# A graph network and expert layer: two buffers for the transposed incidence matrix, compared a graph ahead

## The chip, the cores and the metric

The kernel runs on one core of one Trainium2 chip. The metric is the device time of one execution in microseconds (us). The kernel before takes 750.67 us, the median of 3 runs (749.53 to 751.47). A core has five engines that run side by side and wait for each other by semaphores: PE (TensorE, matrix products), DVE (VectorE), ACT (ScalarE), POOL (GpSimd) and SP (SyncE, which here only starts DMA transfers).

## The reference, cut to what matters

For each of 16 graphs with 512 nodes and 256 features, two layers follow each other. H is the incidence matrix: 1 where adj is not 0.

```
def hypergraph_conv(x, adj, W, b):
    H = (adj != 0).astype(x.dtype)
    w = adj.reshape(N, -1)[:, :C]                     # first row of adj
    xw = einsum('ncd,hd->nch', x, W)
    Dn = 1 / einsum('nce,ne->nc', H, w)               # 0 where the sum is 0
    Be = 1 / H.sum(axis=1)
    m = Be[:, :, None] * einsum('nce,nch->neh', H, xw)
    return Dn[:, :, None] * einsum('nce,neh->nch', H, m) + b

gnn:  h = layer_norm(relu(hypergraph_conv(xn, adj, W1, b1)))      # xn = layernorm(x)
      x1 = x + hypergraph_conv(h, adj, W2, b2) + xn
ffn:  x2 = layernorm(x1)
      logits = x2 @ router_w + router_b; top 2 of 4 experts, softmax -> mask
      comb = sum_e mask_e * silu(x2 @ expert_w_e + expert_b_e)
      y = x2 + comb @ out_w + out_b
      out = x1 + norm_w * y / sqrt(mean(y*y) + 1e-6)
```

## The kernel before, in words

One graph is one pass of `body`. Its 512 nodes are four tiles of 128 rows. Every float32 factor is split in two float16 parts (names that end in h and l, for high and low): ACT writes the high part from PSUM, DVE the low part, and PE multiplies the pairs. H stands in SBUF as `h16` and its transpose as `ht16`, both float16. DVE makes them by comparing the loaded `adjin` and `adjtin` with 0 (`prep_h`, L741, and `prep_ht`, L745).

`body(g)` is a pipeline of two stages: it does the graph network (conv) of graph g and the expert layer (ffn) of graph f = g - 1, and prepares x and H of graph g + 1. `steps` (L221) writes out bodies 0, 1, 2 and the last one, and a hardware loop runs 3 to 14. The order on each engine is the order in which its `body` is written; there is no scheduler. Every engine runs its own list and waits for semaphores.

On PE, one body is in this order: the degrees (L1393, the first instruction of a graph), A1 = H^T times xn (L1405), D = H times w (L1418, the first that needs `ht16` of this graph), the transposes of x2 with the two halves of A2 = H times A1 between them (L1363, L1375), the router (L1440 to L1443), experts 0 and 1, A3 = A2 times W1 with the transposes of the mask after its third tile, expert 2, the mask's rows (L1308, which need the copy `mt` by ACT, L512), the other experts mixed with transposes and V = h times W2, the output product, U = H^T times V (with `h16`) and B3 = H times U (L1346, the last reader of `ht16`).

On DVE a body begins with x1 of graph f (L974) and its statistics, then `prep_ht(g)`, then the low part of A1 (`a1l`, L902), the output rows `yf` of an earlier graph, `xtl` (the low part of the turned x2, L1032), the small steps of D and of the router, and the mask. Near its end stand `xsl`, y, the low part of U (`ul`, L1132) and `prep_h(g + 1)`.

On SP (L256 to L274) the loads and copies of a body are queued in this order: x of the next graph into `xin`, adj into `adjin` once `h16` is made, the transposed adj into `adjtin` once `ht16` is made, `out` from x1, the copy of `xn` into `xb`, and the constant out_b into `x2o`. `xb` is a sum that is gathered by POOL's DMAs: xn, plus x, plus b2, plus vadd, and DVE reads it for x1. ACT's `prep_x` (L435), which writes the next graph's `xn` over the old one, waits until the copy of `xn` has landed.

Of the kernel before, what the change touches and what calls it, by code (L numbers as in the profile page):

```python
# [47 lines left out]
def build(nc, x, adj, adjt, wrow, w1t, b1, gamma, beta, w2t, b2, rw, rb, ew, eb, ow, ob, nw, out):  # L48
# [4 lines left out]
    CG = 2  # L53
    assert (C, D, DH, NE) == (512, 256, 512, 4)

    with ExitStack() as ctx:
# [60 lines left out]
        h16 = sb("h16", [P, CT, C], F16)  # L117
        ht16 = sb("ht16", [P, CT, C], F16)
        wcur = sb("wcur", [P, CT, 4], BF16)
# [101 lines left out]
        def steps(eng, body, tail):  # L221

            body(eng, 0, conv=True, ffn=False, late=False, prep=True)
            body(eng, 1, conv=True, ffn=True, late=False, prep=True)
            body(eng, 2, conv=True, ffn=True, late=True, prep=True)
# [10 lines left out]
        def _(sp):  # L236
# [18 lines left out]

            def body(sp, g, conv, ffn, late, prep):  # L256
                if prep:
                    sp.wait_ge(xn_dn, 4 * g + 4)
                    sp.dma_start(xin[:, :, :], x[g + 1]).then_inc(x_in, 16)
                    sp.wait_ge(h_made, g + 1)  # L260
                    sp.dma_start(adjin[:, :, :], adj[g + 1].rearrange("(t p) e -> p t e", p=P)).then_inc(adj_in, 16)
                    sp.wait_ge(ht_made, g + 1)
                    sp.dma_start(adjtin[:, :, :], adjt[g + 1].rearrange("(t p) c -> p t c", p=P)).then_inc(adjt_in, 16)
# [25 lines left out]
        def _(gp):  # L289
# [94 lines left out]

            def body(gp, g, conv, ffn, late, prep):
                f, q = g - 1, g - 2
# [45 lines left out]
        def _(act):  # L432
# [124 lines left out]

            def body(act, g, conv, ffn, late, prep):
                f = g - 1
# [163 lines left out]
        def _(dve):  # L723
# [18 lines left out]

            def prep_ht(g):
                dve.wait_ge(adjt_in, 16 * g + 16)
                TS(ht16[:, :, :], adjtin[:, :, :], 0.0, None, ALU.not_equal).then_inc(ht_made, 1)  # L745

# [246 lines left out]

            def body(dve, g, conv, ffn, late, prep):
                f, q = g - 1, g - 2
# [8 lines left out]
                if conv:  # L1004
                    if ffn:
                        prep_ht(g)
                    if not ffn:
                        prep_ht(0)
                        largest(a_turn, slice(W1, W1 + 1), 0, a_top)
                        setup_mag_b()  # L1010
# [245 lines left out]
        def _(pe):  # L1256
# [109 lines left out]

            def a2_half(g, half, ffn):

# [4 lines left out]
                for d in range(KD):  # L1373
                    for k in range(CG * half, CG * half + CG):
                        mm(bank[A2_BANK[d]][:, :], a1h[:, k, P * d:P * d + P], ht16[:, k, :],  # L1375
                           start=(k == 0), stop=False)
                        ins = mm(bank[A2_BANK[d]][:, :], a1l[:, k, P * d:P * d + P], ht16[:, k, :],
                                 start=False, stop=(k == CT - 1))
                    if half == 1:
                        ins.then_inc(a2_rdy, 1)  # L1380

            def body(pe, g, conv, ffn, late, prep):
                f = g - 1
                if conv:
# [31 lines left out]
                    for t in range(CT):  # L1416
                        for k in range(CT):
                            ins = mm(bank[D_BANK][:, 4 * t:4 * t + 4], ht16[:, k, P * t:P * t + P], wcur[:, k, :],  # L1418
                                     start=(k == 0), stop=(k == CT - 1))
# [7 lines left out]
                if conv:  # L1427
                    a2_half(g, 0, ffn)
                if ffn:
                    turned_x2(f, 1)  # L1430
                if conv:
                    a2_half(g, 1, ffn)
# [67 lines left out]
                if conv:  # L1500

                    incidence(g, B3_BANK, ht16, uh, ul, u_lo, 4, b3_rdy)

# [136 lines left out]
```

## Time and profile before

| what | value |
| --- | --- |
| median of 3 runs | 750.67 us (749.53 to 751.47) |
| the profiled execution | 751.47 us, of which the span is 749.9 us |
| busy in the span | PE 705.3 us (94%), DVE 652.2 (87%), ACT 495.0 (66%), POOL 288.4 (38%) |
| mean granted clock of PE | 0.985 of full speed |
| chain that ended last | DVE 29%, PE 26%, DMA 14% (DMA xb<-xn alone 13%), ACT 13%, issue 12% |

The span runs from the first to the last instruction; the rest of the run's time lies around it. The end of a matrix product is modelled in the trace, so two products in a row overlap in it; the distance between the starts of two products is the exact thing. A product of 512 columns follows the one before after 0.216 us, one of 256 columns after 0.109 us. In rows of a timeline the last bracket tells how long the engine was idle before the instruction and what ended that.

### The profile page before, as it was taken

What the parts mean: (1) busy time and instruction counts of PE and PEld (TensorE: products, weight loads), DVE (VectorE), ACT (ScalarE), POOL (GpSimd) and SP (SyncE); (2) the same over time, 40 slices, a digit from 0 to 9 for tenths busy, and PEclk for the clock granted to TensorE, in tenths of its full rate; (3) what the DMA queues carried; (4) which work ended last, traced back from release to release, by engine and by line L of the source; (5) the groups of instructions that cost most, each with busy time, mean ns of one, the idle gap of its engine ahead of it and who ended that gap; (6) DMA issues with size and microseconds to landing.
All of it is one profiled execution on the core that took longest, in us unless ns stands there. A gap on an engine that the chain in (4) does not pass through costs nothing.

```text
span 749.9 us, 16620 instructions
## 1 busy us (share of the span) xinstructions
PE 705.3 (94%) x5573; PEld 482.4 (64%) x5573; DVE 652.2 (87%) x1569; ACT 495.0 (66%) x971; POOL 288.4 (38%) x670
## 2 busy tenths in 40 slices
PE   4787999999999999999999999999999999999983
PEld 3364584766758486675858577584857768585671
DVE  4878888889898989989898899988899998988776
ACT  4655757667594856758585766858576685847562
POOL 4223334144353525444351434435153453524242
PEclk9988999999999999999999999999999999999997
DMA  8455538376583838657393765738385664727312
GB/s 290 169 110 201 113 89 239 67 225 131 162 178 94 240 64 229 135 172 164 90 245 60 237 122 182 154 105 231 62 247 111 202 134 129 184 64 184 58 29 56
DMA packets 42584, 111.65 MB, mean 149 GB/s; under 512 B 4160, under 2 KB 5312, under 8 KB 42560
## 3 DMA queue, kind: packets, MB, share of 16 engines
q0 software_dynamic: 13536, 41.42, 30.4%
q1 hardware_dynamic: 29024, 69.92, 28.3%
q8 instruction: 14, 0.23, 0.1%
q14 instruction: 10, 0.08, 0.0%
HBM read 69.91 MB, written 16.25 MB: 115 GB/s over the span
## 4 chain that ended last, share of the span: by engine, by line
DVE 29%; PE 26%; DMA 14%; ACT 13%; issue 12%; POOL 2%; SPq 2%; DVEq 0%; POOLq 0%; ACTq 0%
DMA xb<-xn 13%; PE bank L1261 5%; DVE comb L863 4%; PE bank L1263 4%; PE bank L1262 4%; PE bank L1346 4%; PE bank L1347 4%; DVE silu L859 4%; DVE hntl L878 3%; DVE z L867 3%; DVE ybn L980 2%; DVE x L974 2%; DVE h L741 2%; DVE ht L745 2%; ACT xsh L449 2%
## 5 line engine op out<-in xcount | busy, mean ns | idle before, releaser
L1261 PE MATMUL bank<-xth,ewh 128*128 128x512 f16 (+1 forms) x272 | 100.6, 370 | 2.1 <-DVE ewl L782 2.1
L1263 PE MATMUL bank<-xth,ewl 128*128 128x512 f16 (+1 forms) x272 | 100.7, 370 | 0.0
L1262 PE MATMUL bank<-xtl,ewh 128*128 128x512 f16 (+1 forms) x272 | 100.7, 370 | 0.0
L507 ACT ACTIVATE silu<-bank,ebcol,ksc 128x512 f32<-128x512 f32 x120 | 92.1, 769 | 7.3 <-PE bank L1263 7.2
L1261 PE MATMUL bank<-w2h,hnth 128*128 128x256 f16 x256 | 70.7, 276 | 3.3 <-DVE hntl L878 2.6
L1263 PE MATMUL bank<-w2h,hntl 128*128 128x256 f16 x256 | 70.5, 275 | 0.0
L1262 PE MATMUL bank<-w2l,hnth 128*128 128x256 f16 x256 | 70.5, 275 | 0.0
L548 ACT ACTIVATE a1h<-bank,be 128x256 f16<-128x256 f32 x64 | 26.8, 469 | 54.3 <-PE bank L1406 51.0
L654 ACT ACTIVATE uh<-bank,be 128x256 f16<-128x256 f32 x64 | 26.8, 470 | 53.4 <-PE bank L1347 53.4
L525 ACT ACTIVATE hnth<-bank 128x512 f16<-128x512 f32 x64 | 37.9, 592 | 33.3 <-PE bank L1315 33.3
L1405 PE MATMUL bank<-xsh,h 128*128 128x256 f16 x256 | 58.3, 277 | 0.9 <-DVE xsl L764 0.9
L372 POOL TENSOR_TENSOR yme<-yms,epsrms 128x4 f32<-128x4 f32 (+1 forms) x17 | 3.8, 224 | 143.7 <-ACT ysq L542 136.1
L1346 PE MATMUL bank<-uh,ht 128*128 128x256 f16 x256 | 56.9, 273 | 1.6 <-DVE ul L1132 1.6
L1406 PE MATMUL bank<-xsl,h 128*128 128x256 f16 x256 | 58.2, 277 | 0.0
L1346 PE MATMUL bank<-vh,h 128*128 128x256 f16 x256 | 56.9, 273 | 1.3 <-DVE vl L883 1.3
L1347 PE MATMUL bank<-vl,h 128*128 128x256 f16 x256 | 56.9, 273 | 0.0
L1347 PE MATMUL bank<-ul,ht 128*128 128x256 f16 x256 | 56.9, 273 | 0.0
L863 DVE TENSOR_TENSOR comb<-comb,silu 128x1024 f32<-128x1024 f32 x45 | 54.9, 1219 | 0.5
L859 DVE TENSOR_TENSOR silu<-silu,bank 128x1024 f32<-128x1024 f32 x45 | 54.6, 1214 | 0.0
L520 ACT ACTIVATE hn<-r,hnb,hrs 128x512 f32<-128x512 f32 x64 | 51.8, 809 | 2.7 <-POOL hnb L324 2.6
L1132 DVE SCALAR_TENSOR_TENSOR ul<-bank,be,uh 128x256 f16<-128x256 f32 x64 | 28.0, 480 | 27.8 <-ACT uh L654 27.8
L867 DVE SCALAR_TENSOR_TENSOR z<-bank,dna,b1b 128x512 f32<-128x512 f32 x64 | 46.7, 748 | 4.7 <-PE bank L1263 2.2
(248 smaller groups left out, 2138.3 us busy)
## 6 DMA issues: line engine op xcount, KB each, us to landing
adjin<-adj SPq DMA_DIRECT2D x16, 1024.0 KB, 5.3
adjtin<-adjt SPq DMA_DIRECT2D x16, 1024.0 KB, 6.2
xin<-x SPq DMA_DIRECT2D x16, 512.0 KB, 4.2
xb<-xn SPq DMA_DIRECT2D x16, 512.0 KB, 8.5
xb<-x POOLq DMA_DIRECT2D x16, 512.0 KB, 8.7
xb<-b POOLq DMA_DIRECT2D x16, 512.0 KB, 5.4
xb<-vadd POOLq DMA_DIRECT2D x16, 512.0 KB, 4.5
out<-x SPq DMA_DIRECT2D x15, 512.0 KB, 6.8
```

Source lines behind the costliest of these rows:

```text
L507: af(silu[:, i % 4, :], bank[E_BANK[i]][:, :], ACT.Silu, bias=ebcol[:, i:i + 1], scale=ksc[:, 2:3]).then_inc(silu_dn, 1)
L520: af(hn[:, t, :], r[:, t, :], ACT.Identity, bias=hnb[:, t:t + 1], scale=hrs[:, t:t + 1]).then_inc(hn_dn, 1)
L859: TT(src, src, m, ALU.mult).then_inc(comb_st, 1)
L863: TT(comb[:, :, :], comb[:, :, :], silu[:, 2 * (e % 2):2 * (e % 2) + 2, :], ALU.add).then_inc(comb_st, 1)
L867: STT(z[:, t, :], bank[A3_BANK[t]][:, :], dna[:, t:t + 1], b1b[:, :], ALU.mult, ALU.add).then_inc(z_dn, 1)
L1261: mm(outp, lh, rh, start=first, stop=False)
L1262: mm(outp, lh, rl, start=False, stop=False)
L1263: return mm(outp, ll, rh, start=False, stop=last)
L1346: mm(b, weights[:, k, P * e:P * e + P], hi[:, k, :], start=(k == 0), stop=False)
L1347: ins = mm(b, weights[:, k, P * e:P * e + P], lo[:, k, :], start=False, stop=(k == CT - 1))
L1405: mm(b, h16[:, k, P * e:P * e + P], xsh[:, k, :], start=(k == 0), stop=False)
L1406: ins = mm(b, h16[:, k, P * e:P * e + P], xsl[:, k, :], start=False, stop=(k == CT - 1))
```

## The change

There are now two buffers `ht16`, one for even and one for odd graphs, and `prep_ht(g + 1)` stands near the end of body g, ahead of `ul`, in place of `prep_ht(g)` near the beginning of body g. `body` gets an argument `odd`; the loop's pass now does two graphs (3 and 4, 5 and 6, ...), with six passes in place of twelve. On SP the copy of `xn` and the store of x1 stand ahead of the load of `adjtin`. PE's router waits for the first half of `xtl` and, ahead of its third tile, for the second.

```diff
-            with eng.Fori(3, N - 1) as g:
-                body(eng, g, conv=True, ffn=True, late=True, prep=True)
-            body(eng, N - 1, conv=True, ffn=True, late=True, prep=False)
+            with eng.Fori(3, N - 2, 2) as g:
+                body(eng, g, 1, conv=True, ffn=True, late=True, prep=True)
+                body(eng, g + 1, 0, conv=True, ffn=True, late=True, prep=True)
+            body(eng, N - 1, 1, conv=True, ffn=True, late=True, prep=False)
...
                     sp.wait_ge(h_made, g + 1)
                     sp.dma_start(adjin[:, :, :], adj[g + 1].rearrange("(t p) e -> p t e", p=P)).then_inc(adj_in, 16)
+                if ffn:
+                    f = g - 1
+                    sp.wait_ge(x1_dn, 4 * f + 4)
+                if conv:
+                    if not prep:
+                        sp.wait_ge(xn_dn, 4 * g + 4)
+                    sp.dma_start(xb[:, :, :], xn[:, :, :]).then_inc(xn_kept, 16)
+                if ffn:
+                    sp.dma_start(out[f], x1[:, :, :]).then_inc(x1_st, 16)
+                if prep:
                     sp.wait_ge(ht_made, g + 1)
                     sp.dma_start(adjtin[:, :, :], adjt[g + 1].rearrange("(t p) c -> p t c", p=P)).then_inc(adjt_in, 16)
-                if ffn:
-                    f = g - 1
-                    sp.wait_ge(x1_dn, 4 * f + 4)
-                    sp.dma_start(out[f], x1[:, :, :]).then_inc(x1_st, 16)
-                if conv:
-                    sp.wait_ge(xn_dn, 4 * g + 4)
-                    sp.dma_start(xb[:, :, :], xn[:, :, :]).then_inc(xn_kept, 16)
...
-                    if ffn:
-                        prep_ht(g)
...
                 if ffn and prep:
                     y_part(f, 0)
+                if prep:
+                    prep_ht(g + 1, 1 - odd)
                 if conv:
                     for e in range(CT):
...
-                    pe.wait_ge(xt_lo, 2 * f + 2)
                     for t in range(CT):
+                        if t % CG == 0:
+                            pe.wait_ge(xt_lo, 2 * f + t // CG + 1)
```

SP's order in the third body (graph 2), before; `xn_dn`, `h_made`, `ht_made` and `x1_dn` are the semaphores that ACT or DVE raise when `xn`, `h16`, `ht16` and x1 are written:

```order
L259 DMA xin<-x 128x1024 [waits xn_dn]
L261 DMA adjin<-adj 128x4x512 [waits h_made]
L263 DMA adjtin<-adjt 128x4x512 [waits ht_made]
L267 DMA out<-x 128x1024 [waits x1_dn]
L270 DMA xb<-xn 128x1024 [waits xn_dn]
L274 DMA x2o<-ob 128x1024 [waits y_dn]
```

The same body of SP in the changed kernel:

```order
L260 DMA xin<-x 128x1024 [waits xn_dn]
L262 DMA adjin<-adj 128x4x512 [waits h_made]
L269 DMA xb<-xn 128x1024 [waits x1_dn]
L271 DMA out<-x 128x1024
L274 DMA adjtin<-adjt 128x4x512 [waits ht_made]
L278 DMA x2o<-ob 128x1024 [waits y_dn]
```

The copy of `xn` moved past the load of `adjtin` and the store of x1, and it is held by x1 alone where it stood behind `ht_made`.

DVE at the end of the third body, before (`u_hi` is raised by ACT's high part of U, `x2o_dn` and `o_rdy` belong to y):

```order
L764 SCALAR_TENSOR_TENSOR xsl<-xn,xsh 128x1024 [waits xs_hi]
L896 SCALAR_TENSOR_TENSOR y<-bank,ksc,x2o 128x512 [waits x2o_dn,o_rdy]
L1132 SCALAR_TENSOR_TENSOR ul<-bank,be,uh 128x256 [waits u_hi]
L1132 SCALAR_TENSOR_TENSOR ul<-bank,be,uh 128x256
L1132 SCALAR_TENSOR_TENSOR ul<-bank,be,uh 128x256 [waits u_hi]
```

The same place of DVE in the changed kernel:

```order
L768 SCALAR_TENSOR_TENSOR xsl<-xn,xsh 128x1024 [waits xs_hi]
L900 SCALAR_TENSOR_TENSOR y<-bank,ksc,x2o 128x512 [waits x2o_dn,o_rdy]
L749 TENSOR_SCALAR ht_odd<-adjtin 128x2048 [waits adjt_in]
L1136 SCALAR_TENSOR_TENSOR ul<-bank,be,uh 128x256 [waits u_hi]
L1136 SCALAR_TENSOR_TENSOR ul<-bank,be,uh 128x256
L1136 SCALAR_TENSOR_TENSOR ul<-bank,be,uh 128x256 [waits u_hi]
```

The comparison of the transposed matrix for the next graph now stands between y and `ul`; it has left its place between the statistics of x1 and `a1l`.

## Rows read from the trace of the kernel before

**Rows 1.** Busy time of each engine in graphs 3 to 14: us, busy (instructions), PEclk.

```profile
151.35:671.92 520.57, 515.76 (x4131) 353.72 (x4129) 473.09 (x1129) 359.28 (x708) 210.16 (x481) 1.00 0.62 156
```

**Rows 2.** PE's timeline, first instruction of graphs 2, 8, 9, 15: start us, us.

```profile
106.52 0.44 PE L1393 MATMUL bank<-one,h 128*128 128x1 f16 x12
...
368.55 0.49 PE L1393 MATMUL bank<-one,h 128*128 128x1 f16 x14
...
411.54 0.42 PE L1393 MATMUL bank<-one,h 128*128 128x1 f16 x11
...
671.92 0.44 PE L1393 MATMUL bank<-one,h 128*128 128x1 f16 x12
```

**Rows 3.** PE's timeline, first mask row of graphs 8 and 9.

```profile
387.33 0.38 PE L1308 MATMUL bank<-mt,sel 128*128 128x512 f16 x1
...
431.21 0.39 PE L1308 MATMUL bank<-mt,sel 128*128 128x512 f16 x1 [0.54 <-ACT mt L512]
```

**Rows 4.** ACT's timeline, next graph's xn in graphs 8 and 9.

```profile
381.55 1.09 ACT L442 ACTIVATE xn<-xin,xnb,xrs 128x256 f32<-128x256 f32 x2
...
425.60 1.09 ACT L442 ACTIVATE xn<-xin,xnb,xrs 128x256 f32<-128x256 f32 x2 [1.08 <-DMA xb<-xn]
```

**Rows 5.** Who waited for whom: us in total, times, longest us.

```profile
ACT xn L442 <- DMA xb<-xn: 5.8, 9, 1.1
...
PE bank L1261 <- DVE hntl L878: 2.6, 12, 0.6
```

**Rows 6.** SP's timeline in graph 8.

```profile
372.40 0.38 SPq L263 DMA_DIRECT2D adjtin<-adjt  x1
...
373.49 0.48 SPq L270 DMA_DIRECT2D xb<-xn  x1
```

**Rows 7.** DVE's timeline in the first part of graph 8.

```profile
369.18 0.84 DVE L974 SCALAR_TENSOR_TENSOR x<-bank,dnb,xb 128x256 f32<-128x256 f32 x2
...
371.18 1.19 DVE L745 TENSOR_SCALAR ht<-adjtin 128x2048 f16<-128x2048 f32 x1
...
373.86 0.87 DVE L902 SCALAR_TENSOR_TENSOR a1l<-bank,be,a1h 128x256 f16<-128x256 f32 x2
...
376.10 1.27 DVE L1032 SCALAR_TENSOR_TENSOR xtl<-bank,xth 128x512 f16<-128x512 f32 x2
```

**Rows 8.** PE's timeline in graph 8, last product of A2 and first of the router.

```profile
376.99 0.38 PE L1377 MATMUL bank<-ht,a1l 128*128 128x512 f16 x1
377.43 0.18 PE L1261 MATMUL bank<-rwh,xth 128*128 128x4 f16 x1
```

**Rows 9.** Timelines of graph 1: PE at D, ACT at x2, PE at expert 0.

```profile
60.96 0.55 PE L1418 MATMUL bank<-wcur,ht 128*128 128x4 bf16 x16 [1.14 <-DVE ht L745]
...
62.56 1.09 ACT L555 ACTIVATE x<-x,ynb,yrs 128x256 f32<-128x256 f32 x2 [1.12 <-POOL ynb L324]
...
70.32 0.61 PE L1261 MATMUL bank<-xth,ewh 128*128 128x512 f16 x1 [2.08 <-DVE ewl L782]
```

**Rows 10.** Line 270, the copy of xn into xb, all 16.

```profile
DMA to landing us min/median/max: 3.9/8.5/10.2
```

**Rows 11.** ACT's timeline in graph 8, second pair of a1h.

```profile
372.64 0.84 ACT L548 ACTIVATE a1h<-bank,be 128x256 f16<-128x256 f32 x2
```

**Rows 12.** POOL's timeline in graph 8, the same step for both halves of x1.

```profile
369.34 0.19 POOL L319 TENSOR_TENSOR yve<-ymv,epsln 128x2 f32<-128x2 f32 x1 [0.43 <-DVE ymv L984]
...
371.34 1.08 POOL L319 TENSOR_TENSOR yve<-ymv,epsln 128x2 f32<-128x2 f32 x1 [0.60 <-DVE ymv L984]
```

**Rows 13.** DVE's timeline at the end of graph 7, around the new place.

```profile
361.51 0.74 DVE L896 SCALAR_TENSOR_TENSOR y<-bank,ksc,x2o 128x512 f32<-128x512 f32 x1
363.50 0.88 DVE L1132 SCALAR_TENSOR_TENSOR ul<-bank,be,uh 128x256 f16<-128x256 f32 x2 [1.25 <-ACT uh L654]
```

**Rows 14.** DMA queues: packets, MB, share; and an issue: count, KB, us to landing.

```profile
q8 instruction: 14, 0.23, 0.1%
...
wf<-wrow SPq DMA_DIRECT2D x1, 32.0 KB, 1.9
```

More of the change, by code:

```diff
@@ L53, in build @@
     CG = 2
-    assert (C, D, DH, NE) == (512, 256, 512, 4)
+    assert (C, D, DH, NE) == (512, 256, 512, 4) and N % 2 == 0
     with ExitStack() as ctx:
@@ L221, in steps @@
         def steps(eng, body, tail):
-            body(eng, 0, conv=True, ffn=False, late=False, prep=True)
-            body(eng, 1, conv=True, ffn=True, late=False, prep=True)
-            body(eng, 2, conv=True, ffn=True, late=True, prep=True)
-            with eng.Fori(3, N - 1) as g:
-                body(eng, g, conv=True, ffn=True, late=True, prep=True)
-            body(eng, N - 1, conv=True, ffn=True, late=True, prep=False)
+            body(eng, 0, 0, conv=True, ffn=False, late=False, prep=True)
+            body(eng, 1, 1, conv=True, ffn=True, late=False, prep=True)
+            body(eng, 2, 0, conv=True, ffn=True, late=True, prep=True)
+            with eng.Fori(3, N - 2, 2) as g:
+                body(eng, g, 1, conv=True, ffn=True, late=True, prep=True)
+                body(eng, g + 1, 0, conv=True, ffn=True, late=True, prep=True)
+            body(eng, N - 1, 1, conv=True, ffn=True, late=True, prep=False)
             tail(eng)
@@ L254, in _, with body @@
                 sp.dma_start(dst, src).then_inc(c_in, 16)
-            def body(sp, g, conv, ffn, late, prep):
+            def body(sp, g, odd, conv, ffn, late, prep):
                 if prep:
@@ L383, in _, with body @@
             prep_x(0, again=False)
-            def body(gp, g, conv, ffn, late, prep):
+            def body(gp, g, odd, conv, ffn, late, prep):
                 f, q = g - 1, g - 2
@@ L556, in x2_part, with body @@
                        scale=yrs[:, t:t + 1]).then_inc(x2_dn, 1)
-            def body(act, g, conv, ffn, late, prep):
+            def body(act, g, odd, conv, ffn, late, prep):
                 f = g - 1
@@ L741, in prep_h, with prep_ht @@
                 TS(h16[:, :, :], adjin[:, :, :], 0.0, None, ALU.not_equal).then_inc(h_made, 1)
-            def prep_ht(g):
+            def prep_ht(g, odd):
                 dve.wait_ge(adjt_in, 16 * g + 16)
-                TS(ht16[:, :, :], adjtin[:, :, :], 0.0, None, ALU.not_equal).then_inc(ht_made, 1)
+                TS(ht16[odd][:, :, :], adjtin[:, :, :], 0.0, None, ALU.not_equal).then_inc(ht_made, 1)
             def prep_x_stats(g, tiles=range(CT)):
@@ L992, in degrees, with body @@
                 v.reciprocal(be[:, :], dmax[:, :]).then_inc(be_dn, 1)
-            def body(dve, g, conv, ffn, late, prep):
+            def body(dve, g, odd, conv, ffn, late, prep):
                 f, q = g - 1, g - 2
@@ L1365, in turned_x2, with a2_half @@
                 ins.then_inc(xt_rdy, 1)
-            def a2_half(g, half, ffn):
+            def a2_half(g, odd, half, ffn):
                 pe.wait_ge(a1_lo, 4 * g + CG * half + CG)
@@ L1374, in a2_half @@
                     for k in range(CG * half, CG * half + CG):
-                        mm(bank[A2_BANK[d]][:, :], a1h[:, k, P * d:P * d + P], ht16[:, k, :],
+                        mm(bank[A2_BANK[d]][:, :], a1h[:, k, P * d:P * d + P], ht16[odd][:, k, :],
                            start=(k == 0), stop=False)
-                        ins = mm(bank[A2_BANK[d]][:, :], a1l[:, k, P * d:P * d + P], ht16[:, k, :],
+                        ins = mm(bank[A2_BANK[d]][:, :], a1l[:, k, P * d:P * d + P], ht16[odd][:, k, :],
                                  start=False, stop=(k == CT - 1))
@@ L1380, in a2_half, with body @@
                         ins.then_inc(a2_rdy, 1)
-            def body(pe, g, conv, ffn, late, prep):
+            def body(pe, g, odd, conv, ffn, late, prep):
                 f = g - 1
@@ L1427, in body @@
                 if conv:
-                    a2_half(g, 0, ffn)
+                    a2_half(g, odd, 0, ffn)
                 if ffn:
@@ L1431, in body @@
                 if conv:
-                    a2_half(g, 1, ffn)
+                    a2_half(g, odd, 1, ffn)
                     if not ffn:
```

12 lines of the change are left out of this document (6 added, 6 removed).

## The prediction

> **What bounds the kernel now.** I read the busy times by stage first, then PE's timeline at the start of each graph, then what stands in front of PE's pauses, then the engines and transfers behind those.
>
> PE runs at its full level, 2.4 GHz, through graphs 3 to 14 and is busy for 515.8 of 520.6 us [rows 1]. So only what removes a pause of PE counts there, and the pauses are few. Two graphs show it: graph 8 begins at 368.55 and graph 9 at 411.54, a period of 42.99 us, and from graph 2 to graph 15 the mean is (671.92 - 106.52) / 13 = 43.49 [rows 2]. The slower graphs lose at one place above all. In graph 9 the first mask row on PE comes after an idle 0.54 us, waiting for ACT's copy mt [rows 3]. In graph 8 the same row has no pause. The reason is on ACT: its xn starts 13.00 us after the start of graph 8, and 14.06 after the start of graph 9, where it waited 1.08 for the copy xb<-xn to land [rows 2, 4]; mt stands behind xn in ACT's order. Nine graphs wait so, for 5.8 us together [rows 5]. The copy is late since it is issued at 373.49, behind the load that waits for ht [rows 6].
>
> Two small pauses are in every graph. Between the last product of A2 (376.99) and the router (377.43) lie 0.44 us, 0.22 more than a product takes: PE waits for xtl, which DVE ends at 376.10 + 1.27 = 377.37 [rows 7, 8]. The other is the wait of V for hntl, short each time [rows 5]. Graph 1 has larger ones: 1.14 for ht and 2.08 for ewl, both from DVE [rows 9].
>
> **The copy of xn.** The last x1 on DVE ends at 369.18 + 0.84 = 370.02 [rows 7]. SP can issue the copy about 0.3 later, at 370.3, 3.2 us earlier than now [rows 6], and ahead of 1.5 MB that stand before it now. Even the slowest landing of the 16, 10.2 us, brings it to 380.5 [rows 10]; with the median, 8.5, it is there at 378.8. ACT wants it at 381.2 (below). So the wait goes in every graph, with 0.7 us left in the worst case. Behind it on SP stand the store of x1, the load of adjtin and x2o's constant. They go out earlier as well, since ht was made a graph ago. The load of adjtin has until the end of the body, some 30 us.
>
> If all 13 periods from graph 2 on were like graph 8's, they would be 565.40 - 13 x 42.99 = 6.5 us shorter. The first of them, graph 2, also loses to hntl (the longest of those waits is 0.6) [rows 5], which the copy doesn't cause alone; I leave 0.4 with it and take -6.1 (bounds 0 and -6.5).
>
> **The comparison moved away from the start.** It takes 1.19 us of DVE [rows 7]. Little of this arrives further down, since the next wait takes over: the second pair of a1h on ACT ends at 372.64 + 0.84 = 373.48 [rows 11], and the second a1l, which needs it, stands at 373.86 [rows 7], so it can come 0.36 earlier, at 373.5. These 0.36 go on to xtl, to D, to vadd on ACT, to silu, to xn (381.55 becomes 381.2) and to the mask. For the router xtl then ends at 377.01, before PE wants it at 377.21, so its pause of 0.22 goes: 13 x 0.22 = -2.9 us (bounds 0 and -2.9). The wait by halves is a second way to the same 0.22 (the first half of xtl is there 0.6 before the second), and it can't be gained twice.
>
> The mask row gets no new pause with that: against graph 8, which has none [rows 3], PE arrives 0.22 earlier and mt comes 0.36 earlier. The wait for hntl stays: it is a chain of a transpose on PE, ACT's hnth and DVE, which moves with PE. So my floor for a period is 42.99 - 0.22 = 42.77.
>
> POOL shows one more thing: the step yve takes 0.19 us for the first half of x1 and 1.08 for the second, which starts 0.16 after DVE's ht did and ends as that ends [rows 7, 12]. At its new place ht meets no step of POOL in a graph of the loop, so the second half's statistics come 0.9 earlier. This is inside the 0.36, because ACT's a1h pair is next. The Trainium skill has the rule for it (SBUF — State Buffer, Who interferes with whom): a tensor_scalar of DVE in a two-port mode takes the port pair that it shares with GpSimd, and the second comer is blocked until the first is done. The trace agrees, with 1.08 against 0.19. The rule speaks against the change in one place: in graph 0 ht now falls on POOL's issue of xb<-vadd.
>
> **The comparison in its new place.** y ends at 361.51 + 0.74 = 362.25, and ul starts at 363.50 after 1.25 us of idleness, for ACT's uh [rows 13]. The comparison takes 1.19 [rows 7] and fits with some 0.1 left. That idleness is its cover; without it each graph would pay up to 1.1 us, 14 times, and PE's B3 would wait. I take 0, bounds 0 and +0.1 a graph. No one waits for the comparison itself until D of the next graph.
>
> **Graph 1.** D waits 1.14 us for ht, which is now made in body 0. PE can't use all of it, because x2 and ewl are late behind. There the comparison and POOL's blocked steps hold up ACT's x2 by 1.12 [rows 9]; ACT's x2, ewh and xth and DVE's xtl and ewl follow each other without a gap up to PE's 70.32. x2 can start when the second pair of a1h is done, 1.1 us earlier, and ewl ends 1.1 earlier. Value -1.1; bounds 0 and -1.3. PE is at its lower level, 1.2 GHz, after this pause and will be again.
>
> **Graph 0 and the end.** In body 0 the comparison falls in a similar idle gap of DVE. What it can cost is a later xb<-vadd and with it x1 of graph 0: 0 to +0.6; I take 0. The last body's chains are not touched.
>
> **The loop of two graphs.** Fewer returns save nothing that I can see: the last B3 product and the next graph's first instruction on PE follow each other as usual within the loop. I take 0 (a cost is the third rival).
>
> The sum is -6.1 - 2.9 - 1.1 = -10.1 us. From the profiled execution, 751.47 (span 749.9 and 1.6 around it), that is 741.4; it is the slowest of the three shown, and from the median, 750.67, it is **740.6**.
>
> **Rivals.** First, a floor at 42.99: something else of about 0.2 us (hntl's chain, or ul, if the comparison overruns its gap) takes the place of the router's pause. For it speaks that DVE is busy for 473.1 of the 520.6 us [rows 1] and gets its comparison back into the one real gap; against it that the pauses are seen and belong to xtl. Then 740.6 + 2.9 = 743.5.
>
> Second, the copy doesn't come earlier in effect: it now shares the queue with adjin's megabyte, which is issued just before it, and the landing stays near 381.5 to 382.5, or another transfer waits instead. Then -6.1 is lost and part of the router's -2.9: about 748 to 750. Against it speaks that the slowest landing still fits [rows 10].
>
> Third, slower: the loop's code no longer stays with the engines. A graph is (4131 + 4129) / 12 = 688 instructions on PE, so the pass grows to 1,376. The trace shows 14 instruction transfers of 16 KB on q8 over the whole span [rows 14], which is about one pass over the written code and no reload in twelve loop passes. If the doubled pass is past what is kept, the target of each of the 5 returns must be fetched. The shortest landing of a load is 1.9 us [rows 14]; PE and DVE would both pay, one behind the other, 5 x 3.8 = 19, less 5 x 0.7 that hides in DVE's and PE's slack: 740.6 + 15.5 = 756.1. It decides from 12.4 us on, 2.5 a return, since less would only eat the gain.
>
> The Trainium skill (Runtime: NRT & Kernel Launch, Instruction fetch mechanics) says two things here. One: PE's instruction memory holds 2,048 instructions and the others' 512, in blocks of 256; by this the pass fits, and the sum stands. The other: only two lines are kept, and a taken branch out of the two-page window forces a fetch. By that the loop of before, 2.7 pages of PE, would already fetch at every return, and the trace agrees with the first: 14 transfers in all. An estimate from that page puts the new pass at 5.4 of 8 pages, which leaves room, though not plenty.
>
> **Chances.** The forecast has 0.53 (739 to 742.5), the floor at 42.99 0.26 (742.5 to 746), the copy in vain 0.09, a reload of code 0.10, and 0.02 for a gain beyond the bounds. The range 738.5 to 747 holds the first two. About 0.3%, 2.3 us, is what a measurement here can tell from no change. Faster by more than that (under 748.4): the first two, the gain beyond and a third of the copy in vain, 0.84. Within it: 0.06, the rest of that case. Slower: the code, 0.10.
>
> **What would show it.** In the changed profile graphs 2 to 14 should be 42.8 us apart, all alike, with no wait of ACT for xb<-xn and none of PE for mt; the router's first product should follow A2's last after 0.22; the idle gap before ul should be 0.1 in place of 1.25, and the ul rows at the same distance from uh; yve should take 0.19 in both halves; D in graph 1 should have no wait. q8 should have two or three transfers more, as the written code is longer, and none between the loop's first and last pass. I am wrong if periods alternate between two lengths (the returns), or if the wait before B3 for ul has grown.

## The result, and the profile after

The changed kernel takes 742.42 us, the median of 4 runs (741.57 to 744.01), beside 750.9 us (749.53 to 751.47) for 4 runs of the kernel before. The ratio is 0.9892, 95% interval 0.9869 to 0.9914: 8.1 us, or 1.1%, faster. Run once more among the experiments it took 742.57 us, ratio 0.9899 (0.9881 to 0.9916). The profiled execution took 741.57 us with a span of 740.0; it is the fastest of its four, as the profiled 751.47 of before is the slowest of its four.

Graphs 3 to 14, as one stretch (its ends, then the columns of [rows 1]), and PE's first instruction of graphs 2, 8, 9 and 15, which answer to [rows 2]. The last number of such a row is how many of the degree's 16 products the trace has in a row:

```profile
149.33:662.57 513.24, 511.88 (x4131) 355.89 (x4129) 476.75 (x1129) 357.67 (x708) 203.51 (x481) 1.00 0.63 159
```

```profile
106.45 0.54 PE L1397 MATMUL bank<-one,h 128*128 128x1 f16 x16
...
363.23 0.42 PE L1397 MATMUL bank<-one,h 128*128 128x1 f16 x11
...
405.99 0.37 PE L1397 MATMUL bank<-one,h 128*128 128x1 f16 x9
...
662.57 0.39 PE L1397 MATMUL bank<-one,h 128*128 128x1 f16 x10
```

Graph 8 lasts 405.99 - 363.23 = 42.76 us, and so does every graph from 4 on. From graph 2 to graph 15 it is 556.12 us, 9.28 less than before. The rest of the difference between the two profiled executions (751.47 - 741.57 = 9.90) is: the start 0.22 later, graph 0 longer by 1.65 (42.52, now 44.17), graph 1 shorter by 1.94 (51.14, now 49.20), the part from graph 15 on shorter by 0.55 (78.0, now 77.4).

Graph 8 of the changed kernel, in the order of [rows 3, 4, 6, 7, 8]: ACT's xn and mt, the first mask row on PE, SP's queue, DVE's low parts, and A2's last product with the router's first.

```profile
375.74 1.09 ACT L446 ACTIVATE xn<-xin,xnb,xrs 128x256 f32<-128x256 f32 x2
...
380.72 0.57 ACT L516 ACTIVATE mt<-bank 128x512 f16<-128x512 f16 x1
...
381.78 0.38 PE L1312 MATMUL bank<-mt,sel 128*128 128x512 f16 x1
...
364.83 0.48 SPq L269 DMA_DIRECT2D xb<-xn  x1
365.50 0.44 SPq L271 DMA_DIRECT2D out<-x  x1
366.04 0.72 SPq L274 DMA_DIRECT2D adjtin<-adjt  x1
...
368.19 0.88 DVE L906 SCALAR_TENSOR_TENSOR a1l<-bank,be,a1h 128x256 f16<-128x256 f32 x2
...
370.44 1.27 DVE L1034 SCALAR_TENSOR_TENSOR xtl<-bank,xth 128x512 f16<-128x512 f32 x2
...
371.67 0.38 PE L1381 MATMUL bank<-ht_even,a1l 128*128 128x512 f16 x1
371.89 0.17 PE L1265 MATMUL bank<-rwh,xth 128*128 128x4 f16 x1
```

The copy goes out 1.60 us after the graph's start (4.94 before), no row of xn waits for it in any graph, mt is done at 381.29, half a microsecond before PE wants it, and the router follows A2 after 0.22. SP's line L269 now lands in a median of 4.2 us, against 8.5 in [rows 10]:

```profile
DMA to landing us min/median/max: 2.9/4.2/11.0
```

The comparison at its new place on DVE, which answers to [rows 13], and POOL's two steps yve, which answer to [rows 12]:

```profile
398.95 0.74 DVE L900 SCALAR_TENSOR_TENSOR y<-bank,ksc,x2o 128x512 f32<-128x512 f32 x1
399.61 1.22 DVE L749 TENSOR_SCALAR ht_odd<-adjtin 128x2048 f16<-128x2048 f32 x1
400.95 0.88 DVE L1136 SCALAR_TENSOR_TENSOR ul<-bank,be,uh 128x256 f16<-128x256 f32 x2
...
364.12 0.19 POOL L323 TENSOR_TENSOR yve<-ymv,epsln 128x2 f32<-128x2 f32 x1 [0.53 <-DVE ymv L988]
...
366.08 0.19 POOL L323 TENSOR_TENSOR yve<-ymv,epsln 128x2 f32<-128x2 f32 x1 [0.57 <-DVE ymv L988]
```

The gap of 1.25 us is filled, ul starts 2.00 us after y does (1.99 before), and yve takes 0.19 both times. One pause of PE is left in a graph of the loop, ahead of V's fourth tile. The last product of the third tile and the first of the fourth in graph 8:

```profile
394.68 0.27 PE L1267 MATMUL bank<-w2h,hntl 128*128 128x256 f16 x1
395.06 0.28 PE L1265 MATMUL bank<-w2h,hnth 128*128 128x256 f16 x1
```

They start 0.38 us apart, where 0.11 is usual: 0.27 for hntl.

Graph 1, PE's pauses, which answer to [rows 9]: D has none, but ewl's is longer (2.46, before 2.08), since PE arrives there earlier.

```profile
62.63 0.66 PE L1367 MATMUL bank<-ident,x 128*128 128x128 f32 x4 [0.57 <-ACT x L559]
68.05 0.16 PE L1265 MATMUL bank<-rwh,xth 128*128 128x4 f16 x1 [0.71 <-DVE xtl L1034]
71.46 0.61 PE L1265 MATMUL bank<-xth,ewh 128*128 128x512 f16 x1 [2.46 <-DVE ewl L786]
```

### The profile page after: what moved, and what is told of

Read it like the earlier page. It is cut to its first block, busy times and chain, and to the rows that moved or that the text cites. A ratio compares the mean times of both kernels' runs of the same rounds, so it can differ in the third digit from the quotient of the medians.

```text
span 740.0 us, 16405 instructions
## 1 busy us (share of the span) xinstructions
PE 699.6 (95%) x5573; PEld 485.1 (66%) x5573; DVE 656.4 (89%) x1569; ACT 493.0 (67%) x971; POOL 280.5 (38%) x670
## 4 chain that ended last, share of the span: by engine, by line
PE 26%; DVE 21%; issue 18%; POOL 11%; ACT 11%; DMA 9%; SPq 2%; POOLq 1%; DVEq 0%; ACTq 0%
DMA x2o<-ob 8%; PE bank L1350 6%; PE bank L1351 6%; DVE comb L867 5%; DVE silu L863 4%; PE bank L1265 4%; PE bank L1267 3%; PE bank L1266 3%; POOL hrs L326 3%; DVE hntl L882 2%; ACT hn L524 2%; POOL xb L355 2%; DVE x L978 2%; ACT silu L511 2%; POOL hve L323 1%
## 5 line engine op out<-in xcount | busy, mean ns | idle before, releaser
L511 ACT ACTIVATE silu<-bank,ebcol,ksc 128x512 f32<-128x512 f32 x120 | 92.4, 770 | 10.5 <-PE bank L1267 9.7
L882 DVE SCALAR_TENSOR_TENSOR hntl<-bank,hnth 128x512 f16<-128x512 f32 x64 | 44.1, 689 | 9.7 <-ACT hnth L529 9.7
L1265 PE MATMUL bank<-w1h,a2h 128*128 128x512 f16 x128 | 48.5, 379 | 0.3 <-DVE a2l L1046 0.3
L1266 PE MATMUL bank<-w1l,a2h 128*128 128x512 f16 x128 | 48.5, 379 | 0.0
```

Of the source, the lines that this page charges most:

```text
L511: af(silu[:, i % 4, :], bank[E_BANK[i]][:, :], ACT.Silu, bias=ebcol[:, i:i + 1], scale=ksc[:, 2:3]).then_inc(silu_dn, 1)
L882: STT(hntl[:, t, :], bank[HNT_BANK[t]][:, :], HS, hnth[:, t, :], ALU.mult, ALU.subtract).then_inc(hnt_lo, 1)
L1265: mm(outp, lh, rh, start=first, stop=False)
L1266: mm(outp, lh, rl, start=False, stop=False)
```

## The experiments

In each, "loop" is the time from the start of graph 2 to that of graph 15 in the profile (565.40 before, 556.12 in the changed kernel). Each time is the median of 4 to 12 executions, beside the kernel before on the same chip. The first four rows ran on one chip; the fifth, the sixth, PE's loop of four and hntl ahead of the sum on a second; the other four on a third. The medians of before on the three were 750.47, 750.57 and 750.45, so rows of different chips can be compared, with a little less certainty.

| kernel | us | ratio and 95% interval | loop |
| --- | --- | --- | --- |
| the changed kernel again | 742.57 | 0.9899 (0.9881, 0.9916) | 555.92 |
| two buffers alone | 742.26 | 0.9892 (0.9871, 0.9912) | 555.90 |
| SP's order alone | 745.55 | 0.9938 (0.9921, 0.9956) | 559.42 |
| router by halves alone | 750.73 | 1.0009 (0.9996, 1.0021) | 563.99 |
| SP's order and halves, one buffer | 742.77 | 0.9891 (0.9874, 0.9909) | 558.05 |
| loop of two alone | 754.31 | 1.0039 (1.0022, 1.0055) | 569.03 |
| SP's order, halves, loop of two | 743.51 | 0.9915 (0.9897, 0.9934) | 556.54 |
| changed, comparison behind H's | 748.95 | 0.9990 (0.9975, 1.0006) | 562.97 |
| changed, PE's loop of four | 748.94 | 0.9980 (0.9965, 0.9995) | 564.92 |
| changed, hntl ahead of the sum | 745.51 | 0.9933 (0.9918, 0.9948) | 558.68 |
| changed, high parts first | 738.57 | 0.9846 (0.9824, 0.9868) | 552.28 |
| one buffer, high parts first | 739.31 | 0.9858 (0.9833, 0.9883) | 553.23 |

**Two buffers alone.** The changed kernel without SP's new order and without the wait by halves.

```diff
                     sp.dma_start(adjin[:, :, :], adj[g + 1].rearrange(...)).then_inc(adj_in, 16)
+                    sp.wait_ge(ht_made, g + 1)
+                    sp.dma_start(adjtin[:, :, :], adjt[g + 1].rearrange(...)).then_inc(adjt_in, 16)
...
-                        if t % CG == 0:
-                            pe.wait_ge(xt_lo, 2 * f + t // CG + 1)
+                    pe.wait_ge(xt_lo, 2 * f + 2)
```

> The two buffers and the comparison in its new place alone, with two graphs in a pass of the loop; SP's queue order and the router's wait for both halves of xtl stay as before. Theory (the late copy and the router's pause are two separate losses, and DVE's start does not cost PE otherwise): the router's pause of 0.22 goes, since xtl comes 0.34 earlier; D's wait in graph 1 goes; the load of adjtin no longer holds SP, since ht was made a graph ago, so the copy xb<-xn is issued when x1 is there, about 2 us earlier than before, but with the megabytes of adjin and adjtin ahead of it, so some of its nine waits stay. Graphs 2 to 14 about 558 to 561 us against 565.4 before and 556.1 in the changed kernel, the run 743 to 746 us. Rival (the copy's time of issue counts, not what is queued ahead of it): all nine waits of ACT for the copy are gone, the run is within 1 us of the changed kernel's 742.4. Second rival (only SP's order brought the gain): the run stays above 748.

It took 742.26 us, as fast as the changed kernel, with periods of 42.76. The rival holds. SP's queue in graph 8, and the copy's landings:

```profile
361.83 0.39 SPq L262 DMA_DIRECT2D adjin<-adj  x1
362.32 0.45 SPq L264 DMA_DIRECT2D adjtin<-adjt  x1
364.46 0.37 SPq L268 DMA_DIRECT2D out<-x  x1
364.88 0.71 SPq L271 DMA_DIRECT2D xb<-xn  x1
...
DMA to landing us min/median/max: 4.0/8.3/10.2
```

The copy still needs 8.3 us, about as before. But adjtin's load no longer waits for ht, so the copy is issued 364.88 - 362.73 = 2.15 us after the graph's start and lands at 10.5, ahead of the 12.5 at which ACT wants it. The earlier issue alone is enough; the longer landing behind two megabytes of loads costs nothing here.

**SP's order alone**, on the kernel before: the order of the change, of which the lines that moved up are shown.

```diff
...
+                    sp.dma_start(xb[:, :, :], xn[:, :, :]).then_inc(xn_kept, 16)
+                if ffn:
+                    sp.dma_start(out[f], x1[:, :, :]).then_inc(x1_st, 16)
+                if prep:
                     sp.wait_ge(ht_made, g + 1)
                     sp.dma_start(adjtin[:, :, :], adjt[g + 1].rearrange(...)).then_inc(adjt_in, 16)
```

> The kernel before with SP's new order alone: the copy xb<-xn and the store of x1 stand ahead of the load of adjtin. Theory: ACT no longer waits for the copy, the mask row has no pause from it, and all periods from graph 2 on come to the 42.99 us of the better graphs before; the router's pause of 0.22 stays in each. That takes 6 us off: 744 to 745.5 us. In graph 1 the 1.14 at D stay. Rival (the copy is hidden anyway, the gain comes from DVE's start): 749 to 751. Second rival (the load of adjtin, now issued later, becomes late for ht): DVE waits for adjtin at ht and the run is above 751.

745.55 us, and the loop shorter by 5.98, for which the prediction had 6.1. All periods from graph 3 on are 42.98 to 43.01. The router's pause is still there, in graph 4 (202.53 - 202.09 = 0.44):

```profile
202.09 0.38 PE L1380 MATMUL bank<-ht,a1l 128*128 128x512 f16 x1
202.53 0.18 PE L1264 MATMUL bank<-rwh,xth 128*128 128x4 f16 x1
```

**The wait by halves alone**, on the kernel before (the diff of the change's last part).

> The kernel before with the router's wait by halves of xtl alone. Theory: the pause of 0.22 ahead of the router goes in 13 graphs, but in the nine graphs whose copy is late the mask row waits for mt by as much more, so of the 2.9 us about 1 is kept: 749 to 750.5 us, and the periods stay unequal. Rival (the two losses are independent, everything behind PE moves with it): the full 2.9 us, 747.5 to 748. Second rival (the second half of xtl is too late for the third tile): no change, a new pause between the second and third tile of the router.

750.73 us: nothing, in the timed runs (the ratio's interval, 0.9996 to 1.0021, has no room for a gain of 1 us). Who waited for whom, us in total, times, longest, and PE's wait for mt in the kernel before:

```profile
PE bank L1261 <- DVE hntl L878: 4.0, 15, 1.0
PE bank L1308 <- ACT mt L512: 3.9, 9, 0.5
...
PE bank L1308 <- ACT mt L512: 2.3, 6, 0.5
```

The router's pause is gone, and PE waits longer for mt (3.9, before 2.3) and hntl (4.0, before 2.6 [rows 5]) instead: 3.0 us, as much as the pause was worth. Theory's direction held, its last 1 us didn't: the loop is 1.4 shorter in the one profile, the timed runs show none of it. What a late copy holds back can't be gained on PE ahead of it.

**SP's order and the wait by halves together**, one buffer, one graph a pass.

> The kernel before with two parts of the change and without its large one: SP's new order and the router's wait by halves, one buffer for ht, the comparison at its old place at the start of a body, one graph in a pass of the loop. Theory (the two losses of the loop are the copy issued behind the load of adjtin, which the order alone cures, and the second half of xtl, which the wait by halves alone cures; the place of the comparison is only another way to both): all periods from graph 3 on are 42.77 us, as in the changed kernel, and the run takes 742 to 743.5 us. Rival (the comparison's 1.19 us at the start of DVE's body matter further down: mt and hntl come 0.36 later than in the changed kernel and PE now arrives 0.22 earlier): the pause ahead of the mask row or the one for hntl grows by 0.05 to 0.2, periods are 42.82 to 42.97, and the run takes 743 to 745.5 us.

742.77 us: as fast as the changed kernel, without a second buffer and without doubled code. The rival has a part in it: graph 2 takes 43.81, the periods behind it are 42.76 to 43.02, with 0.31 for hntl and now and then 0.07 to 0.2 at the mask row. That is 2.1 us over the loop, half of it in graph 2. Graphs 0 and 1 take 92.40 together here and 93.32 in the changed kernel run again, which gives 0.9 back. The medians, 742.77 and 742.57, don't tell the two kernels apart.

**The changed kernel again.**

> The changed kernel once more, beside its parts. Theory and rival alike: 741.5 to 743.5 us, graphs 2 to 14 in 556.1 us with periods of 42.77. What it is for: the sum of the parts against it on one chip, and whether the 1.65 us that graph 0 took longer (44.17 us against 42.52) come again. If they come from DMA landings at the start (the load that ACT waited 2.08 us for, 0.79 before) they change from run to run; if they come from the comparison in body 0, which falls on POOL's issue of the copy, only about 1.2 of them come again, and in the first kernel of this set too.

Graph 0 took 44.11 us, again 1.6 more than the 42.52 of before. But the kernels in which the comparison stands where it stood took 43.72 (SP's order alone), 43.92 (the halves alone) and even 44.69 (the loop of two alone, below, which has the code of before in its graphs 0 to 2). So the 1.6 can't be put down to the change. One part is PE's wait for the turned magnitudes (they hang on a load at the start): the product that turns them starts 0.38 us after the one ahead of it in the profile of before, and 1.1 to 1.6 us after it in those of the changed kernel (both times) and of its three parts, with or without the second buffer. From the first product of U to the end of graph 0, the stretch in which the comparison now stands, it takes 9.06 or 9.07 us in before, the changed kernel and all its parts. The execution of before that was profiled had a short graph 0.

**The loop of two alone**, on the kernel before.

```diff
-            with eng.Fori(3, N - 1) as g:
+            with eng.Fori(3, N - 2, 2) as g:
                 body(eng, g, conv=True, ffn=True, late=True, prep=True)
+                body(eng, g + 1, conv=True, ffn=True, late=True, prep=True)
```

> The kernel before with two graphs in a pass of the loop and nothing else. Theory (the code stays with the engines, a return costs nothing): 750.0 to 751 us, the interval of the ratio holds 1.000, and three more instruction transfers on q8 than before, as in the changed kernel, some of them in the first pass of the loop. Rival (returns cost, fewer of them save): under 749.5. Second rival (the new code is reloaded each pass): above 752, with transfers on q8 in every pass.

754.31 us, by the medians 3.7 slower, by the ratio 2.9 (its interval is 1.7 to 4.1). No theory had that: the second rival has the time, but with transfers in every pass, and there are none between graph 4 and the last body. The profiled execution, 756.52, is the slowest of its eleven (one took 750.99), so its 3.6 more in the loop need not be those of every execution. It has them in graph 4, the first that runs the added code: 242.41 - 195.50 = 46.91 us. ACT's xn and PE's mask there:

```profile
211.62 1.09 ACT L443 ACTIVATE xn<-xin,xnb,xrs 128x256 f32<-128x256 f32 x2 [3.15 <-DMA xb<-xn]
...
213.70 0.60 PE L1297 MATMUL bank<-ident,m 128*128 128x128 f16 x4 [2.01 <-DVE m L955]
```

And the transfers in flight between 200 and 212 us (packets, MB, share; the copy's us to landing):

```profile
q8 instruction: 1, 0.02, 0.5%
q14 instruction: 1, 0.01, 0.2%
...
xb<-xn SPq DMA_DIRECT2D x1, 512.0 KB, 11.2
```

In the same stretch of the kernel before there is no instruction transfer and the copy lands in 8.5. The copy, which had nothing to spare, was 3.15 us late once, and behind its pause PE was at 1.2 GHz for some 3 us (granted clock 0.50 from 214.1 to 217.0, 0.43 us from one product's start to the next in place of 0.22). That the instruction transfers made it late fits both traces, and the one of two buffers alone, where the copy took 9.6 us in graph 4 and 8.1 to 8.8 in the rest of the loop; shown is only that they coincide.

**The same on the kernel with SP's order and the halves.**

> SP's new order and the wait by halves (742.8 us so far), with two graphs in a pass of the loop. The loop of two alone had cost the kernel before 3.7 us, 3.6 of them in graph 4 in the profile, where the copy xb<-xn landed 11.2 us after its issue. Theory (the first fetch of the added code delays a transfer once, and that costs only where the transfer has nothing to spare; here the copy is issued early): 742 to 743.8 us, graph 4 within 0.3 us of its neighbours. Rival (the added code costs about 3.7 us wherever it stands, and the changed kernel hides that in another gain): 745.5 to 747 us.

743.51 us, 0.7 more than its parent, and graph 4 takes 42.87 us between neighbours of 42.76. The instruction transfers are there, but the copy is issued first and lands in 4.0. So the added code has next to no cost of its own here. That the cost of the loop of two is that of a transfer without slack, and that the changed kernel has the slack, is the reading that fits both.

**The comparison without its cover**: the changed kernel, with `prep_ht(g + 1)` behind `prep_h(g + 1)`.

> The changed kernel with the comparison of the transposed matrix at the very end of DVE's body, behind that of H, where no idle time of DVE covers it. Theory (the gap ahead of ul is the comparison's cover, and DVE has little to spare at the start of a body): the next graph's x1, statistics, a1l and xtl all come later by up to 1.19 us less what idle time there is at the start; a1l's idle 0.44 before it and the 0.2 that the router has to spare take 0.6 of that, and the rest, 0.3 to 0.6 us a graph, comes up ahead of the router or at A2: 746 to 751 us. Rival (the cover does not matter, DVE catches up in its other gaps): within 1 us of 742.4.

748.95 us, 6.4 to 6.5 more than the changed kernel (742.57 and 742.42); the period is 43.31. The size was right, the place wasn't. The pause is neither at the router nor at A2 but ahead of the first turn of x2:

```profile
371.85 0.33 PE L1366 MATMUL bank<-ident,x 128*128 128x128 f32 x1 [0.39 <-ACT x L559]
```

**PE's loop of four**: the changed kernel, PE alone with four graphs in a pass.

```diff
+            if eng is nc.tensor:
+                with eng.Fori(3, N - 4, 4) as g:
+                    for q in range(4):
+                        body(eng, g + q, (1 + q) % 2, conv=True, ffn=True, late=True, prep=True)
```

> The changed kernel with four graphs in a pass of PE's loop (three passes of 2,752 instructions); the other engines keep two graphs in a pass. It asks how near the changed kernel is to the point where the loop's code no longer stays, which was the slower rival of the prediction. Theory A (code beyond what PE keeps is fetched again in each pass, and PE stops for it): transfers on q8 in the second and third pass, pauses of PE of 1.9 us or more that no other engine explains, above 745 us. Theory B (it is fetched again, but ahead of its use, or it still stays): 742 to 743 us and periods of 42.77; transfers on q8 between 330 and 660 us tell the two halves of B apart.

748.94 us, 6.4 more than the changed kernel run again: theory A, though the pauses are shorter than its 1.9 us. PE's first instruction behind the first and the second return (graphs 7 and 11) and a product in graph 7:

```profile
321.86 0.55 PE L1402 MATMUL bank<-one,h 128*128 128x1 f16 x16 [1.66 <-issue]
326.37 0.28 PE L1415 MATMUL bank<-xsl,h 128*128 128x256 f16 x1 [1.21 <-issue]
...
497.55 0.55 PE L1402 MATMUL bank<-one,h 128*128 128x1 f16 x16 [1.62 <-issue]
```

Instruction transfers in the second pass (321.8 to 497.5 us) and in the third (497.5 to 671.1):

```profile
q8 instruction: 13, 0.21, 0.5%
...
q8 instruction: 12, 0.20, 0.5%
```

"Issue" is idle time that no other engine explains. With 2,752 instructions a pass the code is fetched again in each pass; with 1,376, in the changed kernel, not one instruction transfer comes between 235 and 662 us. The three pauses are 4.5 of the 9.0 us by which this profile's loop is longer than that of the changed kernel run again; behind the last of them PE was at 1.2 GHz for some 3 us, and the rest I have not broken down.

**hntl ahead of the last sum**: PE turns h's fourth tile before V's second, DVE writes the fourth hntl before the last sum of the experts.

```diff
+                if conv:
+                    hnt_part(g, 3)
                 if ffn:
                     combine_sum(f, 3)
...
-                    v_tile(g, 1)
                     transposed_h(g, 3)
+                    v_tile(g, 1)
```

> The changed kernel with one pause more attacked: PE turns the fourth tile of h ahead of V's second tile, not behind it, and DVE writes the fourth hntl ahead of the last sum of the experts, not behind it. Theory (the 0.27 us that PE waits for the fourth hntl are DVE's order and PE's turn alone): the fourth hntl ends at about 25.3 us after the graph's start in place of 31.8 less 0.5, so the pause goes in 14 graphs, the period falls from 42.77 to 42.50 and the run to 738.5 to 739.5 us. Rival (the last sum, 1.22 us, is now 0.6 later, and cth on ACT and ctl behind it become late for the output product): the pause moves to the output product and is 0.1 to 0.5, the run is 740 to 745 us.

745.51 us, 3 slower than the changed kernel, and half a microsecond above the rival's range. It is the rival all the same: hntl's pause is gone, and one stands at the output product in each graph, where the starts are 0.48 us further apart than usual (the row's 0.32 counts from the modelled end of the product before):

```profile
398.04 0.28 PE L1266 MATMUL bank<-owh,cth 128*128 128x256 f16 x1 [0.32 <-DVE ctl L893]
```

**High parts first**, on the changed kernel. Nothing moves on DVE or ACT; PE waits for each part where it reads it. The diff shows V's fourth tile; the output product got the same for `cth` and `ctl`.

```diff
-                pe.wait_ge(hnt_lo, 4 * g + t + 1)
+                pe.wait_ge(hnt_hi if t == 3 else hnt_lo, 4 * g + t + 1)
...
+                if t == 3:
+                    for k in range(KH):
+                        mm(b, hnth[:, t, P * k:P * k + P], w2h[:, k, :], start=(k == 0), stop=False)
+                        mm(b, hnth[:, t, P * k:P * k + P], w2l[:, k, :], start=False, stop=False)
+                    pe.wait_ge(hnt_lo, 4 * g + 4)
+                    for k in range(KH):
+                        ins = mm(b, hntl[:, t, P * k:P * k + P], w2h[:, k, :], start=False, stop=(k == KH - 1))
```

> The changed kernel, where PE's fourth tile of V waits for the high part of h only, does its eight products with it, and then waits for the low part (hntl); the output product does the same with cth and ctl. Theory (the last pause of the loop, 0.27 us, is the end of DVE's hntl and nothing else, and the output product wants ctl only about 0.1 us before it is there): no pause of PE is left in graphs 2 to 14, the period is 42.50 us in place of 42.77, and the run is 738.5 to 739.5 us. Rival (as when hntl was written ahead of the last sum, a pause comes up at the output product or ahead of U, since all engines behind it run as late as before): periods of 42.7 or more, 741.5 us or more.

738.57 us, the fastest of all: 3.9 under the changed kernel and 11.9 under the kernel before. Periods are 42.48, and in graphs 3 to 14 PE is busy from the first to the last hundredth:

```profile
148.76:658.56 509.80, 509.80 (x4130) 357.20 (x4128) 476.82 (x1129) 357.75 (x708) 205.89 (x481) 1.00 0.64 160
```

**The same with one buffer.**

> The same on the version without the second buffer: SP's new order, the router's wait by halves, high parts first in the fourth tile of V and in the output product; one ht, the comparison at its old place, one graph in a pass. Its parent ran as fast as the changed kernel, with periods of 42.80 to 43.02. Theory (its pauses are hntl's 0.31 and now and then the mask row's): periods of 42.50 to 42.75, 738.5 to 740.5 us, within 1.5 us of the changed kernel with the same edit. Rival (mt has nothing to spare here, since the comparison still stands at the start, and every graph waits for it once PE is faster): periods of 42.7 to 42.9, 741 to 743 us.

739.31 us, within the intervals of the one above. Its periods are 42.48 too, but for graphs 2 (43.23) and 5 (42.67).

## Why the prediction was right, and where it was not

The forecast was 740.6 us, or 741.4 for the profiled execution, which took 741.57. Between the two profiled executions the sum of -10.1 is met by 9.90. In the timed runs it is 2 us too large: they show 8.1, and the interval, 6.5 to 9.8, leaves 10.1 out. All terms were read from the profiled execution of before, the slowest of its four, and the changed kernel's is the fastest of its four; the other executions have no trace, so which term is smaller in them can only be read from the experiments.

- **The copy of xn, -6.1**: right in mechanism and in the profile, 5.98 in the loop. In the timed runs SP's order alone gives 750.47 - 745.55 = 4.9 (3.3 to 5.9 by the ratio), so about half of the missing 2 us may lie here. The landing, taken as 8.5 us from the rows, is 4.2 with the load of adjtin behind it.
- **The router, -2.9**: the pause is gone in every graph of the loop. What that is worth on top of the early copy, with the comparison at its old place, is less clear. In the timed runs it is 745.55 - 742.77 = 2.8, but in the profiles only 559.42 - 558.05 = 1.4 of it is in the loop and as much in graph 1 (50.11, with the halves 48.79); with a loop of two it is 559.42 - 556.54 = 2.9 in the loop. The condition that I gave, that mt comes 0.36 earlier, was not needed for most of it: once the copy is early, the wait by halves does it, less 0.04 to 0.26 in most graphs, where hntl and mt now hold PE a little. And without the early copy it is worth nothing.
- **Together -9.0 in the loop**, 9.28 measured; the floor 42.77, measured 42.76. Both ends of the chain of 0.36 were seen: xtl starts 7.21 us after the graph's start, before 7.55 [rows 2, 7], and xn 12.51, before 13.00 [rows 2, 4]. The rival of a floor at 42.99 falls.
- **The second buffer** gained nothing of its own that the timed runs show; in the profiles its loop is shorter by 2.1 us, or by 0.6 beside the kernel with SP's order, the halves and the loop of two (556.54). What it does, another route to the same two losses, I had seen for the router only. SP's new order and the new place of the comparison are each enough for the copy.
- **The new place, 0**: right, and the cover is real. Without it a graph pays 0.55, half of the 1.1 that I gave as the bound.
- **Graph 0, 0**: nothing of its 1.6 us is shown to be the change's, as said above. Graphs 0 and 1 together are only 0.3 us shorter between the two profiles (93.67, now 93.37), where the sum had -1.1.
- **Graph 1, -1.1**: the pause at D went, and ewl comes 0.7 earlier after the graph's start, not 1.1. The 1.94 between the two profiles are no measure of it. SP's order alone and the loop of two alone took 50.11 and 50.12 in graph 1, 1.0 less than the profile of before, and the loop of two has the same code there. In the one profile of before PE stayed at 1.2 GHz for 5.5 us behind ewl's pause, in that of SP's order for 3.4:

```profile
70.30:75.80 5.50, 5.48 (x13) 1.96 (x14) 4.59 (x25) 3.71 (x9) 3.73 (x8) 0.50 0.14 27
```

```profile
71.90:75.30 3.40, 3.37 (x8) 1.19 (x9) 3.16 (x17) 2.29 (x5) 1.80 (x6) 0.51 0.00 0
```

Beside those two the changed kernel's 49.20 is 0.9 less, near the 1.1. But that is not the second buffer's alone. Graph 1 takes 49.1 to 49.6 us in five profiles with the second buffer and the halves (without the kernel that lacks the cover), and 48.7 to 48.9 in the four with one buffer and the halves, where D still waits. PE's stretch at 1.2 GHz lies in another place in those four, in A2, where the turned x2 is late anyway. In the five it lies behind ewl's pause, where each of some eight products costs 0.21 more. The stretch in the kernel with the halves alone, and in the changed kernel (columns of [rows 1], the third from the end is the granted clock):

```profile
65.60:68.80 3.20, 3.20 (x11) 1.70 (x10) 1.04 (x3) 2.90 (x4) 0.00 (x0) 0.51 0.98 362
```

```profile
71.50:74.40 2.90, 2.90 (x7) 1.00 (x8) 2.71 (x15) 1.86 (x5) 1.38 (x4) 0.50 0.00 0
```

In the four it comes behind a D that waited, in the five behind a D that did not. That these belong together is likely and was not tried. If so, the second buffer pays at the clock what it gains at D.
- **The loop of two, 0**: right in this kernel (0.7 at most) and wrong as a rule: it cost the kernel before 2.9 to 3.7. I had looked for the price at the returns; it is in the first pass. What I said of q8 held, in count (17, before 14) and in place: the three added transfers fall in graph 4, in the loop's first pass, and none between that and the last body.
- **Code that doesn't stay**: no return costs anything at 1,376 instructions. The mechanism is real at 2,752, at 1.6 to 1.7 us a return, near the 1.9 that I took for one fetch. The Trainium skill (Runtime: NRT & Kernel Launch, Instruction fetch mechanics) gives PE an instruction memory of 2,048 instructions. It also says that a taken branch out of a two-page window forces a fetch. The traces agree with the first, with 25 transfers in the second and third pass of 2,752 and none behind the first pass of 1,376; the changed kernel's returns without a fetch speak against the second.

## What to carry to other kernels

A wait in a queue holds all that stands behind it. Before a buffer is doubled to shorten such a wait, move the transfer that someone needs ahead of the one that waits: here two moved statements and a split wait gave what the second buffer gave, as far as the timed runs can tell. An engine that multiplies high and low parts should wait for each part where it reads it; with that, V's last pause went for nothing, while a reordering of the producers only moved it. Written-out code can have a price in its first pass: here 2.9 to 3.7 us where a transfer had no slack, and 0.7 at most where it had.

## What was not expected of the hardware

Half a megabyte copied within SBUF lands in a median of 4.2 us when it is issued ahead of a load of one megabyte, and in 8.3 to 8.5 behind it. The reader that waits feels only the sum of issue and landing. With the comparison behind H's the copy is issued 2.59 us after the graph's start in place of 1.5 to 1.6 and lands in a median of 3.1, so at 5.7 us as in the changed kernel. The load of adjin, issued ahead of it, lands at 4.5 us in graph 8 of both; that the copy waits for that load's data is likely and was not tried. The first pass over 688 new instructions on PE (three transfers of 16 KB on q8, two on q14) went together with a copy late by 2.7 us. And in the first two graphs the time hangs on where the stretches at 1.2 GHz and the first loads fall: graph 0 took 42.52 us in one profile and 44.69 in another that has the same code there, and graph 1 took 51.14 and 50.12 in the same two. A term of about 1 us there can't be read from two profiles.
